# Last phase of a four-layer graph kernel: x3 turned at the end of a step, source rows normalised a step later, plain pairs over 22 steps

## What is computed

```python
x = _layernorm(x + _L2(x, src, dst, ...), axis=-1)         # update of the rows that are sources, others plain
# last layer, attention over the edges:
q, k, v = jnp.split(x @ W, [512, 1024], axis=-1)           # 8 heads of 64
aw = einsum('ehf,ehf->eh', q[src] * 64**-0.5, k[dst])      # one score per edge and head
e = exp(aw - segment_max(aw, src)[src])
out = segment_sum(e / segment_sum(e, src)[src] * v[dst], src)
x = _layernorm(x + out, axis=-1)
```

## Time and profile before

| What | Value |
|---|---|
| median of 3 runs | 2155.89 us (2150.03 to 2163.36) |
| the profiled execution | 2165.3 us, its span 2163.5 us |
| PE, DVE, ACT, POOL busy | 86%, 67%, 53%, 42% of the span |
| first product of a step to the next step's, middle of the last phase | 23.84 us |
| last phase, from its first gather to the end | 1645.86 to 2163.5 us |

### The profile page before, as it was taken

The page is one execution under the profiler, slowest core; times in us unless marked ns, Lnnn a source line. Parts: engine busy times, 40 slices in busy tenths (PEclk is TensorE's granted clock), DMA queues, the critical chain, the costliest instruction groups (busy, mean ns, idle before and its releaser), DMA issues. The chain is left out here.

```text
span 2163.5 us, 24571 instructions
## 1 busy us (share of the span) xinstructions
PE 1853.0 (86%) x5525; PEld 953.6 (44%) x5525; DVE 1442.2 (67%) x2642; ACT 1157.3 (53%) x2376; POOL 916.6 (42%) x1049
## 2 busy tenths in 40 slices
PE   5999999599999999999999995952881878888885
PEld 2444444244444444444444443521781444444442
DVE  5365555077777777777777774327985687788774
ACT  1344434255555555555555552224884888778772
POOL 2212102156666666666666663444553222232214
PEclk9999999799999999999999998975555887787777
DMA  7752102534444444444444445554556877777743
GB/s 251 246 206 67 25 10 31 141 133 171 171 164 164 158 164 171 171 167 161 167 156 171 171 147 199 98 93 156 113 111 189 244 223 222 223 221 215 225 133 119
DMA packets 165550, 344.68 MB, mean 159 GB/s; under 512 B 30146, under 2 KB 30627, under 8 KB 164966
## 3 DMA queue, kind: packets, MB, share of 16 engines
q1 hardware_dynamic: 130710, 247.28, 32.6%
q0 software_dynamic: 31424, 92.08, 19.0%
q10 hardware_dynamic: 3344, 4.51, 0.7%
HBM read 171.91 MB, written 153.71 MB: 151 GB/s over the span
## 5 line engine op out<-in xcount | busy, mean ns | idle before, releaser
L687 PE MATMUL d_p_h<-w3a,d_xT 128*128 128x512 f32 x632 | 286.4, 596 | 23.1 <-DMA d_xT<-in_xT 23.1
L687 PE MATMUL d_p_o<-d_w,d_uT 128*128 128x512 f32 x632 | 284.5, 593 | 3.0 <-ACT d_uT L762 3.0
L687 PE MATMUL d_p_p<-d_wr,d_x1T 128*128 128x512 f32 x632 | 285.1, 594 | 0.0
L562 POOL TENSOR_SCALAR d_small<-d_mv 128x1 f32<-128x1 f32 x158 | 78.0, 494 | 297.5 <-DVE d_mv L813 149.5
L851 DVE TENSOR_TENSOR d_zz<-d_yg,d_xbeta 128x512 f32<-128x512 f32 x79 | 136.9, 1733 | 96.2 <-POOL d_yg L902 96.2
L687 PEld LDWEIGHTS d_p_h<-w3a,d_xT 128*128 128x128 f32 x632 | 120.9, 192 | 176.0 <-issue 176.0
L687 PEld LDWEIGHTS d_p_o<-d_w,d_uT 128*128 128x128 f32 x632 | 119.8, 190 | 153.8 <-issue 149.2
L755 ACT ACTIVATE d_yn<-d_y,d_small 128x512 f32<-128x512 f32 x79 | 64.3, 814 | 228.4 <-POOL d_small L567 228.4
L1739 PE MATMUL f_p_qv<-filters,same_dst 128*128 128x512 f32 x160 | 126.4, 962 | 66.8 <-ACT same_dst L1819 66.8
L687 PEld LDWEIGHTS d_p_p<-d_wr,d_x1T 128*128 128x128 f32 x632 | 114.5, 191 | 114.4 <-issue 114.4
L783 ACT ACTIVATE d_x<-d_zz,d_small 128x512 f32<-128x512 f32 x79 | 64.2, 813 | 176.6 <-POOL d_small L567 176.6
(11 more groups left out here) (285 smaller groups left out, 4110.3 us busy)
## 6 DMA issues: line engine op xcount, KB each, us to landing
sum_counted<-m_tile_sum SPq DMA_DIRECT2D x10, 2112.0 KB, 7.8
state<-d_empty SPq DMA_DIRECT2D x80, 264.0 KB, 2.4
update<-d_empty SPq DMA_DIRECT2D x80, 256.0 KB, 2.3
pair_x<-x SPq DMA_DIRECT2D x40, 512.0 KB, 4.2
out_rows<-pair_rows SPq DMA_DIRECT2D x40, 512.0 KB, 3.7
d_xT<-in_xT SPq DMA_DIRECT2D x79, 256.0 KB, 2.7
d_z<-sum_counted SPq DMA_DIRECT2D x79, 256.0 KB, 2.8
d_x<-in_x SPq DMA_DIRECT2D x79, 256.0 KB, 3.1
```

The source lines that it names most:

```text
L562: nc.gpsimd.tensor_scalar(tmp, var, factor, add, ALU.mult, ALU.add).then_inc(done, 1)
L687: last = nc.tensor.matmul(out[:, :], lhsT[:, c, :], w[:, c, :], start=(c == 0), stop=(c == KB - 1))
```

## The change

Five things are moved; no instruction is added to or taken from the computation.

- PE: `turn_x3` moves from the start of the step after to the end of the step in which ACT made the x3 rows. `turn_ssp` and `second` move from the step after to the end of the step that made the softplus. The queries are then the first work of a step.
- ACT: `ssp_turned_out`, `x3_turned_out` and `second_product_out` move to the end of a step in the same way.
- ACT: `source_rows` of a tile moves from the end of the step that made its rows to the start of the next one, behind `state_factors` and ahead of the early plain tiles.
- The plan of the pairs: from 2 in each of steps 0 to 19 to 2 in most of steps 0 to 21 and 1 in steps 7, 11, 16 and 20. The last two steps have none.
- POOL: from 8, 9 and 3 tiles of source rows scattered in the last three steps to 8 in the last but one and 12 in the last. The wait for the stores of all plain rows moves one step later with them.

```diff
-    plan = [2] * (steps - 4) + [0] * 4
+    plan = [2] * 4 + [2, 2, 2, 1, 2, 2, 2, 1, 2] * 2 + [0] * 2
...
-        WRITTEN = (0, 8, T - 3, T)
+        WRITTEN = (0, 8, T)
...  (POOL)
-                if step == STEPS - 3:
+                if step == STEPS - 2:
                     for b in range(ROW_BUFS):
                         pool.wait_ge(k.pair_gone[b], 16 * (PAIRS // ROW_BUFS))
-                if step >= STEPS - 3:
-                    for i in range(WRITTEN[step - STEPS + 3], WRITTEN[step - STEPS + 4]):
+                if step >= STEPS - 2:
+                    for i in range(WRITTEN[step - STEPS + 2], WRITTEN[step - STEPS + 3]):
                         scatter_out(i)
...  (ACT)
-                if 0 <= c < T:
-                    x3_turned_out(c, 0)
-                    x3_turned_out(c, 1)
                 if 0 <= e < T:
                     state_factors(e)
-                if 0 <= b < T:
-                    ssp_turned_out(b)
+                if 0 <= e - 1 < T:
+                    source_rows(e - 1)
                 for u in range(unit, unit + early):
                     tile_normalise(nc, k, act, u)
...
-                if 0 <= b < T:
-                    second_product_out(b)
...
-                if 0 <= e < T:
-                    source_rows(e)
+                if a < T:
+                    ssp_turned_out(a)
+                if 0 <= b < T:
+                    x3_turned_out(b, 0)
+                    x3_turned_out(b, 1)
+                if a < T:
+                    second_product_out(a)
                 for u in range(unit + early + between, unit + TILES[step]):
                     tile_normalise(nc, k, act, u)
```

More of the change, by code:

```diff
@@ L1787, in _ @@
             for step in range(STEPS):
-                b, c, d = step - 1, step - 2, step - 3
-                if 0 <= c < T:
-                    turn_x3(c, 0)
-                    turn_x3(c, 1)
-                if 0 <= b < T:
-                    turn_ssp(b)
+                a, b, c, d = step, step - 1, step - 2, step - 3
                 if 0 <= c < T:
@@ L1799, in _ @@
                     turn_scores(d)
-                if 0 <= b < T:
-                    second(b)
-                if 0 <= d < T:
                     spread_scores(d)
@@ L1806, in _ @@
                     keys(c)
+                if a < T:
+                    turn_ssp(a)
+                if 0 <= b < T:
+                    turn_x3(b, 0)
+                    turn_x3(b, 1)
+                if a < T:
+                    second(a)
                 if 0 <= d < T:
```

## The result

The changed kernel took 2236.41 us (median of 4 runs, 2232.99 to 2237.61), the kernel before 2156.65 beside it (4 runs, 2150.03 to 2163.36). The ratio is 1.0367, 95% interval 1.0333 to 1.0401: slower by 80 us.

What follows compares the result with a forecast made beforehand. It took a loop through the queries to bound each 23.84 us step, with a second only 0.7 below. Terms of +3, +30, 0, +12.7 and +17 made +63 on the median 2155.9: about 2218, range 2172 to 2242.

Steps and rivals of the forecast that it cites:

- start of step 4: Last phase up to step 4's spread start: a slower s in one step and a full ACT, +3 us (0 to 5).
- steps 4 to 20: 13 two-pair steps of 26.5 us and 3 one-pair steps of 22.6: 412 against 381.9, +30.
- 21 to 22: Between these spread starts, now with a pair and four tiles on ACT: 25.3 us against 12.6, +12.7.
- step 22 to the end: Eight scatters wait for the last plain store, then state and twelve others: 45.3 us against 28.2, +17 (14 to 18).
- Moves on PE and ACT: In two-pair steps the queries stop bounding; a loop through DVE and ACT does, making the step s + 17.2 us.
- The first loop: Spread, values, weighing, softplus, source_rows, turned x3, queries, ACT's copies: sets the 23.84 us step before; gone after the change.
- the second: Spread, values, weighing, second pair, scores, factors, two tiles, ACT's copies: 23.2 us before; source_rows enters it (+1.61).
- What the clock does to s: s, PE's spread plus values up to DVE's weighing, starts at half clock: 9.3 us (7.0 to 10.5) against 7.36.
- full clock: Rival: PE's one long block keeps the clock up, s 5.6 us, -11 in all, 2145; chance 0.08.
- Sum over the phase: Changes from the phase's start to its end added up: +63 us, the 22 steps of plain work bringing nothing back.
- Present clock: Rival: spread and values cost 7.4 us as now, +25 in all, 2181; chance 0.20 (2170 to 2198).
- Faster: Rival: neither ACT nor DVE waits, steps of 20.3 and 17.5 us, about -42 in all, 2114; chance 0.06.

Runs made afterwards that it cites:

- fourth run: The changed kernel with PE's idle time ahead of each spread filled by matmuls on constants that nobody reads: 2199.22 us, ratio 1.0184.
- eighth: The fourth run with the spread multiplying all 128 rows, 120 of them zeros, in place of 8: 2167.50 us, ratio 1.0019.
- third run: The kernel before with only the new plan of the pairs and the new scatters, old order on PE and ACT: 2198.18 us, ratio 1.0181.
- first run: The changed kernel with source_rows back in its own step, behind ACT's last plain tile: 2211.49 us, ratio 1.0247.
- sixth run: The changed kernel with ACT's copies of queries and scores moved right behind the factors, ahead of source rows and early tiles: 2143.05 us, ratio 0.9884.
- runs 5 and 9: 5: the kernel before with PE's idling ahead of the queries filled, 2171.52 us; 9: the sixth run with the spread on all 128 rows, 2158.26 us.

## Why the prediction was right

The prediction, 2218, was 18 below the measured 2236; this lies inside the range of 2172 to 2242, and each term of the sum can be laid beside its row (the first and the last as differences from before, the others as lengths).

| term | predicted | after |
|---|---|---|
| start of step 4 | +3 | +3.0 |
| steps 4 to 20 | 412 | 415.8 |
| 20 to 21 | 21.9 | 22.5 |
| 21 to 22 | 25.3 | 24.9 |
| step 22 to the end | 45.3 | 46.1 |
| sum, against before's span | +63 | +67.7 |

The first row agrees in part by luck. The phase begins, by its first gather, at 1643.52 after and at 1645.86 before, ahead of all that the change touches; from there to the start of step 4 it is 78.3 against 73.0, +5.3 and not +3.0. The term was an estimate without a sum behind it.

**Moves on PE and ACT: right, and shown.** The first loop went and the second, lengthened by `source_rows`, took its place. From weighing to factors it measures 9.66 (I had 9.67), from factors to spread 7.37 (7.50). The run that took the 1.6 of source rows out cut the idling by 1.60 and the time by 25; the run that moved the copies ahead of all of it gave 93 (87.9 by the spans). Moving work off PE's path was worth nothing while the buffer that it filled lay for 7 us behind source rows and two tiles in ACT's queue.

**What the clock does to s: right in kind, too small by 0.6.** I took 3.5 for the spread and 5.8 for the values; they are 3.78 and 6.18 in the step shown, 9.92 up to the weighing instead of 9.3. That step is 26.95 against 26.5, a one-pair step 23.0 to 23.1 against 22.6. Over steps 4 to 20 the values vary from 5.10 to 6.46, and the mean two-pair step is 26.66, so the 0.6 overstates the miss of the sum. The ratio of the spread at the two levels, 3.78 / 2.05 = 1.84, is close to the 1.87 of the turns in the earlier trace rows. Of the Trainium skill's page "TensorE: Matmul & The Clock Gate" the ratio in the table of Part 1 would have given an estimated 3.9, 0.1 us above the row. The section "Loop structure matters more than you think" of the same page of the Trainium skill says that a copy out of PSUM doesn't break PE's warmth where the next matmuls follow immediately. That condition is not met here: PE waits for the copies, 7.37 ahead of most spreads and 3.55 behind a one-pair step, and from step 4 to 20 the spread takes 3.77 or 3.78 either way. So this case doesn't test what the page says: it was no support for the *full clock*, and the prediction was wrong to write that the trace disagrees with it.

**The cause that I didn't see.** I explained the slow values by the idling alone. The fourth run cut the idling from 7.37 to 1.33 and left them at 5.18 to 6.69 from step 5 on, mostly 5.40; only the eighth, with full rows and the same idling, brought 3.60. So two things cost clock here, idling ahead of the spread and the spread's own 8 rows. My values of 5.30 from the kernel before held part of this, since they stand behind a spread of 8 rows with only 0.28 of idling; that 5.8 came near is in part luck, since I put it down to idling alone. Nor does the cause act in every step: behind 8 rows the values took 3.70 in steps 5 and 21 of the kernel before. With both changed the kernel after is 2167.5, 69 below itself, near what the rival *full clock* had priced (-74), and still not faster than before. The one long block, on which that rival rested, doesn't keep the clock up by itself.

**Sum over the phase: right in the end, one sentence wrong.** "The 22 steps of plain work bring nothing back" holds for the kernel before, where the third run shows 381.9 both times, not for the one after: 436.3 with the old plan, 415.8 with the new. My estimate came out right since it priced the one-pair steps by themselves; 16 steps at my 26.5 would have been 424. And the end is not a constant of the plan: +17.9 after (I had 17), +25.3 in the third kernel (I had 22), where the last tile waits behind `source_rows`. This doesn't need the place that costs 25 in the steps: in the first run `source_rows` stands in its own step behind the last tile, and the end is +18.5.

**The median.** From spans the loss is 67.7, from medians 80. Before's profiled execution lay above all its timed runs and after's was the lowest; the other 12 are that scatter, 8.7 (2165.3 - 2156.65) and 3.4 (2236.41 - 2232.99), and no term of mine. Of the miss of 18 the terms make 4.7.

**The other rivals.** *Present clock* (2181) fell with the measured s. *Faster* (2114) needed the copies not to be behind 7.5 of queue; the sixth run made just that true and came to 2143, with steps of 19.4 to 23.4 where I had written 20.3 and 17.5, because ACT's weights, behind tiles and logarithms, then came late for the weighing, and softplus behind it.

## What to carry to other kernels

Before a wait on a producer is removed, read when the consumer's engine gets to the result: in an in-order queue a finished buffer behind two long items is as late as an unfinished one, and here moving two copies up in ACT's queue was worth 93 us, more than the change cost. Making an engine faster moves its idling to the next wait, and if the clock falls there, what stands behind that wait pays (runs 5 and 9); so ask of each gain where the idling goes, and what runs right behind it. An item taken out of one step to shorten it gains only if the next steps don't pay it back: compare sums over several steps, as the third run shows.

## What the runs showed of the hardware

- With the same idling ahead, 1.32 in most steps, the values take mostly 5.40, 5.18 to 6.69 from step 5 to 20, behind a spread on 8 of 128 rows (fourth run) and 3.60 behind the same spread with 120 rows of zeros (eighth run), at a granted clock of 0.91 against 1.00 from 1750 to 2050. The zeros cost nothing on PE: 2.05 both ways. With 8 rows the clock does not fall in every step: the values took 3.70 in steps 5 and 21 of the kernel before and in four steps of the sixth. What decides it stays open.
- Idling of 4.40 or more ahead of the spread left it at 3.77 or 3.78, 0.28 to 1.33 at 2.05 in most steps; between them, from 1.56 to 3.72, anything from 2.02 to 3.78 occurred.
- The steps fall into few lengths: 27.3 in thirteen steps running with the old plan, 24.4 and 26.1 with the filled idling, 23.2 and 18.4 with the clock up from step 4 to 20. The fourth kernel has a 26.1 every four or five steps behind the same idling; there the spread takes 2.4 to 2.7 and the values 6.4 to 6.7. Why, stays open.
